# Mamba scan: y summed by tokens with accumulating fp32 transposes, the gate applied by tokens, and one token tile of each state scaled on VectorE

## The chip, the core and the metric

The kernel runs on one core of a Trainium2 chip. Its metric is the device time of one execution in microseconds (us). TensorE multiplies and transposes, VectorE (DVE in the rows), ScalarE (ACT) and GpSimd (POOL) work on 128 partitions at a time, SyncE (SP) issues the DMAs. PSUM, the memory that TensorE writes, has 8 banks of 512 fp32 per partition.

## The reference, cut to what matters

Two layers on x of 2 x 1024 x 256: attention and a gated feed-forward, then a Mamba block and a sparse feed-forward. The change is in the Mamba block, whose core is a scan over the 1024 tokens for each of 512 channels and 16 states:

```
x, z = split(h @ in_proj.T)                  # x, z: [b, 1024, 512]
x_conv = silu(conv4(x))
delta  = softplus(... + bias)                # [b, 1024, 512]
deltaA = exp(delta * A)                      # one A per channel and state
dBu    = delta * B[token, state] * x_conv
for each token:  h = deltaA * h + dBu ;  y = sum over the 16 states of h * C[token, state]
y = y + x_conv * D
y = y * silu(z)
out = y @ out_proj.T
```

## The kernel before, in words

Each engine has a program written out by hand; engines wait for each other by semaphores. After attention and the first feed-forward, each of the two batches b goes through `mamba_pre` (projections, convolution, softplus), `mamba_scan`, and a stretch behind the scan in which the output projection of b and the x projection of the next batch alternate. The sparse feed-forward comes last.

A scan works in channel tiles of 128 partitions x 1024 tokens. It has two halves of two channel tiles each (`half`, and `e` = 0, 1 inside it), and in each half 16 states, four (`v` = 0 to 3) in each of four iterations `it`. So a batch has 32 pairs of states; a pair is one state for both `e`. I call one (`v`, `e`) a step. A step passes through five operations:

- `spread` (ScalarE): u, kept by tokens in `m_uT` (tokens on partitions), is scaled by B of this state, one instruction of 256 channels for each of the 8 token tiles, into `m_uB`. One `spread` serves both `e`. Semaphore `ub_done`.
- `expand` (TensorE, L939): 8 transposes turn `m_uB` back to channels x tokens, into the PSUM banks 4+2e and 5+2e (`drive(e)`, one buffer for each `e`). It waits for the scan that read the same two banks. Semaphore `db_done`.
- `decays` (ScalarE, L1470): exp(delta * A) of 1024 tokens into `m_da`. Semaphore `da_done`.
- the scan (VectorE, L2238): h of 1024 tokens into one of the four `m_h` buffers, from `m_da` in SBUF and `drive(e)` in PSUM. Semaphore `scan_done`.
- the product with C (GpSimd, L2494), in place in `m_h`, semaphore `hc_done`; then `add_state` (TensorE, L946) adds it to y in PSUM by two matmuls of 512 columns with the identity as the weights (the trace has two records for each), banks 2e and 2e+1, semaphore `y_added`.

TensorE's order is `expand(v, e)`, `add_state(v-1, e)`, `expand(v, e+1)`, `add_state(v-1, e+1)`. When a half is done, VectorE forms y + D*x_conv (`dve_mamba_skip`, L2269), the product with silu(z) (`dve_mamba_gate`, L2275), ScalarE takes the high part (`act_y_hi`, L1504) and VectorE the low part (`dve_mamba_y_lo`, L2279) for the output projection `pe_mamba_out` (L984). For the first half these stand between the states of the second half; for the second half they come behind the scan.

## Time and profile before

| | us |
|---|---|
| median of 3 runs (1726.64 to 1728.74) | 1728.73 |
| the profiled execution, its own time | 1728.79 |
| its span in the trace | 1727.0 |
| first to last product with C, batch 0 | 1140.15 to 1312.79 |
| start of the sparse feed-forward on TensorE | 1577.21 |

Read it so: about 1.8 us lie outside the span. The two scans take a fifth of the span. Nothing ahead of 1108 us is touched by the change.

### The profile page before, as it was taken

Reading aid. Unit: us, or ns where it says so; the run is one execution under the profiler, and the core shown is the slowest. Engines: PE = TensorE matmul, PEld = TensorE weight load, DVE = VectorE, ACT = ScalarE, POOL = GpSimd, SP = SyncE. Lnnn points to the kernel's source line nnn. Section 1 sums busy time; section 2 is a strip of 40 time slices with the busy share of each in tenths; the row PEclk is TensorE's granted clock in tenths of the full one; section 3 lists DMA queues with packets and bytes.
Section 4 is the critical chain, followed back from the end, with each engine's and each line's share of the span. In section 5 each row is a group of like instructions: output and inputs, shape, how many; then the busy total and the mean of one; then the engine's idle time right before and its main releaser. Section 6 shows DMA issues by size and latency. Waiting matters only on the chain.

```text
span 1727.0 us, 31389 instructions
## 1 busy us (share of the span) xinstructions
PE 1649.3 (96%) x9564; PEld 1366.6 (79%) x9564; DVE 1394.7 (81%) x2319; ACT 1267.8 (73%) x2380; POOL 765.0 (44%) x717
## 2 busy tenths in 40 slices
PE   8999999999999999999997899789999899999998
PEld 7899889998999889989996788556557656557887
DVE  7788878887787778777876667878888788888997
ACT  5777777777777777777774555799996899984442
POOL 4444445443545354445442111059883079881000
PEclk9999999999999999999999999989999999999999
DMA  3000000000000000000000000023220022240000
GB/s 99 32 20 19 28 27 18 18 30 24 16 16 28 24 15 15 27 24 15 22 0 16 35 0 0 4 87 108 94 89 13 18 108 97 98 142 5 13 13 25
DMA packets 25105, 64.13 MB, mean 37 GB/s; under 512 B 2832, under 2 KB 8976, under 8 KB 24784
## 3 DMA queue, kind: packets, MB, share of 16 engines
q1 hardware_dynamic: 25040, 63.31, 10.8%
q8 instruction: 36, 0.59, 0.1%
q14 instruction: 29, 0.24, 0.0%
HBM read 60.94 MB, written 2.36 MB: 37 GB/s over the span
## 4 chain that ended last, share of the span: by engine, by line
PE 63%; POOL 18%; DVE 10%; issue 6%; ACT 2%; DMA 1%; POOLq 0%; DVEq 0%; SPq 0%; ACTq 0%
POOL m_h L2494 16%; PE ps L567 11%; PE ps L529 10%; PE ps L552 7%; PE ps L484 7%; PE ps L580 5%; PE ps L507 5%; PE ps L802 4%; PE ps L709 3%; PE ps L814 2%; PE ps L730 2%; POOL prob L2364 1%; PE ps L984 1%; POOL prob L2357 1%; DVE m_delta L2175 1%
## 5 line engine op out<-in xcount | busy, mean ns | idle before, releaser
L2494 POOL TENSOR_TENSOR m_h<-m_h,m_C 128x1024 f32<-128x1024 f32 x128 | 309.6, 2424 | 161.4 <-DVE m_h L2238 161.0
L2238 DVE TENSOR_TENSOR_SCAN m_h<-m_y,ps 128x1024 f32<-128x1024 f32 x128 | 291.0, 2283 | 44.9 <-PE ps L939 41.8
L2364 POOL TENSOR_SCALAR prob<-prob,rinv 128x128 f32<-128x128 f32 (+7 forms) x256 | 229.2, 903 | 212.7 <-DVE rinv L1655 206.2
L2357 POOL TENSOR_SCALAR prob<-prob 128x128 f32<-128x128 f32 (+7 forms) x256 | 188.4, 736 | 285.5 <-ACT prob L1077 277.0
L946 PE MATMUL ps<-m_h,ident 128*128 128x512 f32 x512 | 246.0, 603 | 11.2 <-POOL m_h L2494 11.1
L1621 DVE TENSOR_TENSOR pt_lo<-ps,pt_hi 128x512 fp32r<-128x512 f32 (+2 forms) x320 | 189.4, 604 | 81.0 <-ACT pt_hi L1090 79.2
L1614 DVE CUSTOM_DVE_ANT_0 prob<-prob,bias 128x128 f32<-128x128 f32 (+7 forms) x256 | 213.9, 853 | 7.9 <-POOL prob L2357 4.7
L1077 ACT ACTIVATE prob<-ps 128x128 f32<-128x128 f32 (+7 forms) x256 | 165.9, 653 | 67.2 <-PE ps L529 66.6
L1090 ACT ACTIVATE pt_hi<-ps 128x512 fp32r<-128x512 f32 (+2 forms) x320 | 162.9, 531 | 66.5 <-PE ps L552 64.5
L1464 ACT ACTIVATE m_u<-m_uT,m_bT 128x256 f32<-128x256 f32 x512 | 210.7, 497 | 0.1
L1083 ACT ACTIVATE prob<-prob,nmax 128x128 f32<-128x128 f32 (+7 forms) x256 | 198.2, 776 | 3.0 <-DVE nmax L1614 2.0
L939 PEld LDWEIGHTS ps<-ident,m_u 128*128 128x128 f32 x1024 | 122.6, 143 | 74.0 <-issue 59.8
L552 PE MATMUL ps<-ident,prob 128*128 128x128 f32 x1152 | 159.5, 274 | 7.4 <-POOL prob L2364 4.2
L552 PEld LDWEIGHTS ps<-ident,prob 128*128 128x128 f32 x1152 | 135.3, 141 | 29.2 <-issue 7.2
L946 PEld LDWEIGHTS ps<-m_h,ident 128*128 128x128 f32 x512 | 88.1, 192 | 79.8 <-issue 63.8
L529 PE MATMUL ps<-qk_hi 128*128 128x512 f32 (+2 forms) x384 | 143.4, 373 | 4.5 <-DVE v_lo L1627 2.4
L939 PE MATMUL ps<-ident,m_u 128*128 128x128 f32 x1024 | 136.4, 277 | 7.1 <-DVE m_uT L2226 5.0
L1470 ACT ACTIVATE m_y<-m_delta,negA 128x1024 f32<-128x1024 f32 x128 | 139.3, 1137 | 0.0
L529 PE MATMUL ps<-qk_hi,qk_lo 128*128 128x512 f32 (+2 forms) x384 | 131.9, 344 | 0.0
L529 PE MATMUL ps<-qk_lo,qk_hi 128*128 128x512 f32 (+2 forms) x384 | 131.3, 342 | 0.0
L567 PE MATMUL ps<-pt_hi,v_hi 128*128 128x512 f32 (+2 forms) x320 | 116.4, 364 | 0.0
L567 PE MATMUL ps<-pt_lo,v_hi 128*128 128x512 f32 (+2 forms) x320 | 115.7, 362 | 0.0
(263 smaller groups left out, 3960.2 us busy)
## 6 DMA issues: line engine op xcount, KB each, us to landing
m_C<-bc_dram SPq DMA_DIRECT2D x64, 512.0 KB, 3.6
wqk_raw<-wqk_in SPq DMA_DIRECT2D x16, 512.0 KB, 3.2
wv_raw<-wv_in SPq DMA_DIRECT2D x16, 256.0 KB, 2.6
wo_raw<-wo_in SPq DMA_DIRECT2D x16, 256.0 KB, 2.8
q_raw<-wgu_in SPq DMA_DIRECT2D x8, 256.0 KB, 2.7
raw<-wgu_in SPq DMA_DIRECT2D x1, 2048.0 KB, 8.1
out<-x SPq DMA_DIRECT2D x8, 256.0 KB, 2.1
x<-x_in SPq DMA_DIRECT2D x2, 512.0 KB, 4.4
```

The costliest lines, as they stand in the source:

```text
L529: mm = nc.tensor.matmul(flat[:, o + lo_c:o + hi_c], (qk_hi, qk_lo)[a][:, 2 * u, qt * P:(qt + 1) * P], (qk_hi, qk_lo)[w][:, 2 * u + 1, lo_c ...
L552: mm = nc.tensor.transpose(ps[:, 4 + idx % 2, r * P:(r + 1) * P], prob[:, at:at + P], ident[:, :])
L567: mm = nc.tensor.matmul(ps[:, 6 + g, c0:BANK], (v_hi, v_lo)[w][:, j, u * DH:(u + 1) * DH], cols, start=(j == 0 and i == 0), stop=(j == 4 * ...
L939: mm = nc.tensor.transpose(ps[:, 4 + 2 * e + t // 4, (t % 4) * P:(t % 4 + 1) * P], m_uB[:, v % 2, t, e * P:(e + 1) * P], ident[:, :])
L946: mm = nc.tensor.matmul(ps[:, 2 * e + c, :], ident[:, :], m_h[:, 2 * (v % 2) + e, c * BANK:(c + 1) * BANK], start=begin, stop=end)
L1083: nc.scalar.activation(prob[:, at:at + n], prob[:, at:at + n], ACT.Exp, bias=nmax[:, k:k + 1], scale=-1.0, accum_out=rsum[:, k:k + 1]).the ...
L1464: nc.scalar.activation(m_uB[:, v % 2, t, :], m_uT[:, half, t, :], ACT.Copy, scale=m_bT[:, t, bass.ds(it * RING + v, 1)]).then_inc(ub_done, 1)
L1614: nc.vector.tensor_tensor_reduce(out=tile, in0=tile, in1=bias[:, k // 8, S - n:S], scale=-1.0, scalar=BIG, op0=ALU.add, op1=ALU.min, accum ...
L2238: nc.vector.tensor_tensor_scan(m_h[:, 2 * (v % 2) + e, :], m_da[:, 2 * (v % 2) + e, :], drive(e), 0.0, ALU.mult, ALU.add).then_inc(scan_do ...
L2357: nc.gpsimd.tensor_scalar(prob[:, at:at + n], prob[:, at:at + n], CLIP, -CLIP, ALU.min, ALU.max).then_inc(s_clipped, 1)
L2364: nc.gpsimd.tensor_scalar(prob[:, at:at + n], prob[:, at:at + n], rinv[:, k:k + 1], 1.0, ALU.mult, ALU.mult).then_inc(norm_done, 1)
L2494: nc.gpsimd.tensor_tensor(state, state, m_C[:, v, :], ALU.mult).then_inc(hc_done, 1)
```

## The change

**What it does.** y is summed by tokens. `add_state` is now 8 transposes (tokens x 128 channels) that accumulate in PSUM (`is_transpose=True`, `start=False`), into blocks `y_block(t, e)` that fill banks 0 to 3. Ahead of them `begin_y` puts D*x_conv there by 8 transposes for each `e`; the product D*x_conv is made by GpSimd in four instructions at the start of `pool_mamba_scan`. silu(z) is made by tokens: `pe_in_z` has the x tokens as the weights. The gate is one multiplication of PSUM by `m_zT` for two banks, after both `e` are complete. Then `pe_y_turn` turns y back by 8 transposes for each channel tile into PSUM, from which ScalarE takes the high part and VectorE the low part. `spread` makes 7 tiles; the eighth (`spread_last`) is made by VectorE.

```diff
             def add_state(half, it, v, e, end=False):
                 pe.wait_ge(hc_done, unit(b, half, it, v, e) + 1)
-                for c in range(2):
-                    mm = nc.tensor.matmul(ps[:, 2 * e + c, :], ident[:, :],
-                                          m_h[:, 2 * (v % 2) + e, c * BANK:(c + 1) * BANK],
-                                          start=begin, stop=end)
+                for t in range(TILES):
+                    mm = nc.tensor.matmul(y_block(t, e), m_h[:, 2 * (v % 2) + e, t * P:(t + 1) * P], ident[:, :],
+                                          start=False, stop=end and e == 1 and t % 2 == 1, is_transpose=True,
+                                          skip_group_check=True)
                 mm.then_inc(y_added, 1)
+            def begin_y(half):
+                for e in range(2):
+                    pe.wait_ge(xd_done, DT * b + 2 * half + e + 1)
+                    for t in range(TILES):
+                        nc.tensor.matmul(y_block(t, e), m_xc[:, 2 * half + e, t * P:(t + 1) * P], ident[:, :],
+                                         start=e == 0 and t % 2 == 0, stop=False, is_transpose=True,
+                                         skip_group_check=True)
...
+            for v in range(RING):
+                if v == 2:
+                    for e in range(2):
+                        pe.wait_ge(scan_done, unit(b, 1, 1, v, e) + 3)
+                        pe_y_turn(pe, b, e)
+                        add_state(1, 1, v - 1, e)
+                for e in range(2):
+                    if v == 2:
+                        pe.wait_ge(y_lo, DT * b + e + 1)
+                    expand(1, 1, v, e)
...
+        def pe_y_turn(pe, b, e):
+            at = y_bank(b, e)
+            for t in range(TILES):
+                mm = nc.tensor.transpose(ps[:, at + t // 4, (t % 4) * P:(t % 4 + 1) * P],
+                                         m_yT[:, e // 2, t, (e % 2) * P:(e % 2 + 1) * P], ident[:, :])
+            mm.then_inc(yt_full, 1)
...
-            pe_in_x(pe, 1, range(4))
-            pe.wait_ge(y_skip, DT)
-            pe_mamba_out(pe, 0, (0, 1))
+            pe_in_x(pe, 1, range(2))
+            pe.wait_ge(yz_done, 3)
+            pe_mamba_out(pe, 0, (0, 1), range(4))
+            pe.wait_ge(yz_done, 4)
+            pe_y_turn(pe, 0, 2)
+            pe.wait_ge(m_in_read, 16 + 4)
+            pe_y_turn(pe, 0, 3)
+            pe_mamba_out(pe, 0, (0, 1), range(4, TILES))
+            pe.wait_ge(y_lo, 3)
+            pe_in_x(pe, 1, range(2, 4))
+            pe_mamba_out(pe, 0, (2,))
+            pe.wait_ge(y_lo, 4)
             pe_in_x(pe, 1, range(4, 8))
-            pe_mamba_out(pe, 0, (2,))
             pe_mamba_out(pe, 0, (3,))
             pe_mamba_pre(pe, 1)
             pe_mamba_scan(pe, 1)
-            pe.wait_ge(y_skip, 2 * DT - 1)
+            pe.wait_ge(yz_done, 8)
+            pe_y_turn(pe, 1, 2)
+            pe_y_turn(pe, 1, 3)
+            pe.wait_ge(y_lo, 8)
             pe_sparse_turn(pe, 0)
...
-                for t in range(TILES):
+                for t in range(TILES - 1):
                     nc.scalar.activation(m_uB[:, v % 2, t, :], m_uT[:, half, t, :], ACT.Copy,
                                          scale=m_bT[:, t, bass.ds(it * RING + v, 1)]).then_inc(ub_done, 1)
...
+            def spread_last(half, it, v):
+                dve.wait_ge(db_done, unit(b, half, it, v, 0) + 2)
+                dve.sem_inc(seen, 1)
+                nc.vector.tensor_scalar(m_uB[:, v % 2, TILES - 1, :], m_uT[:, half, TILES - 1, :],
+                                        m_bT[:, TILES - 1, bass.ds(it * RING + v, 1)], None,
+                                        ALU.mult).then_inc(ub_last, 1)
...
+        def dve_mamba_gate(dve, b, half, c):
+            dve.wait_ge(y_added, 8 + (2 * b + half + 1) * HALF_UNITS)
+            nc.vector.tensor_tensor(m_yT[:, half, 4 * c:4 * c + 4, :],
+                                    ps[:, 2 * c:2 * c + 2, :].rearrange("p a (t n) -> p (a t) n", t=2),
+                                    m_zT[:, half, 4 * c:4 * c + 4, :], ALU.mult).then_inc(yz_done, 1)
...
         def pool_mamba_scan(pool, b):
+            for e in range(DT):
+                pool.wait_ge(m_sp, 5 * DT * b + 3 * DT + 2 * e + 2)
+                nc.gpsimd.tensor_scalar(m_xc[:, e, :], m_xc[:, e, :], skip_d[:, e:e + 1], None,
+                                        ALU.mult).then_inc(xd_done, 1)
```

**How the instructions move.** First TensorE at the start of a scan. In these rows `m_u` is the memory of `m_uB`, and a transpose has the data as its weights. Before:

```order
L939 MATMUL ps<-ident,m_u 128x128 [waits ub_done,scan_done,ut1_read]
L939 MATMUL ps<-ident,m_u 128x128 [waits ub_done] x7
L939 MATMUL ps<-ident,m_u 128x128 [waits scan_done]
L939 MATMUL ps<-ident,m_u 128x128 x7
L939 MATMUL ps<-ident,m_u 128x128 [waits ub_done,scan_done]
L939 MATMUL ps<-ident,m_u 128x128 [waits ub_done] x7
L946 MATMUL ps<-m_h,ident 128x512 [waits hc_done]
L946 MATMUL ps<-m_h,ident 128x512
```

And now, from the second row on:

```order
L967 MATMUL ps<-ident,m_u 128x128 [waits ub_done] x6
L967 MATMUL ps<-ident,m_u 128x128 [waits ub_last]
L967 MATMUL ps<-ident,m_u 128x128 [waits scan_done]
L967 MATMUL ps<-ident,m_u 128x128 x7
L985 MATMUL ps<-ident,m_xc 128x128 [waits xd_done]
L985 MATMUL ps<-ident,m_xc 128x128 x7
L985 MATMUL ps<-ident,m_xc 128x128 [waits xd_done]
L985 MATMUL ps<-ident,m_xc 128x128 x7
L967 MATMUL ps<-ident,m_u 128x128 [waits ub_done,scan_done]
L967 MATMUL ps<-ident,m_u 128x128 [waits ub_done] x6
L967 MATMUL ps<-ident,m_u 128x128 [waits ub_last]
L975 MATMUL ps<-ident,m_h 128x128 [waits hc_done]
```

Every sum of a step has gone from two matmuls of 512 columns to eight transposes of 128, and 16 transposes of D*x_conv stand ahead of the third `expand`.

Second, TensorE in the second half, at the turn of the first half's y (states 5 and 6 of the second half), now:

```order
L1048 MATMUL ps<-ident,m_xc 128x128 [waits scan_done]
L1048 MATMUL ps<-ident,m_xc 128x128 x7
L975 MATMUL ps<-ident,m_h 128x128 [waits hc_done]
L975 MATMUL ps<-ident,m_h 128x128 x7
L1048 MATMUL ps<-ident,m_xc 128x128 [waits scan_done]
L1048 MATMUL ps<-ident,m_xc 128x128 x7
L975 MATMUL ps<-ident,m_h 128x128 [waits hc_done]
L975 MATMUL ps<-ident,m_h 128x128 x7
L967 MATMUL ps<-ident,m_u 128x128 [waits ub_done,scan_done,y_lo]
```

The two turns write the banks of `drive(0)` and `drive(1)`, so the next `expand` stands behind `y_lo`. Before, nothing of y passed through TensorE here.

Third, VectorE around the first half's y. Before:

```order
L2238 SCALAR_TENSOR_TENSOR m_h<-m_y,ps 128x1024 [waits db_done,y_added,da_done] x6
L2275 TENSOR_TENSOR m_xc<-m_xc,m_z 128x1024 [waits y_skip]
L2238 SCALAR_TENSOR_TENSOR m_h<-m_y,ps 128x1024 [waits db_done,y_added,da_done] x4
L2275 TENSOR_TENSOR m_xc<-m_xc,m_z 128x1024 [waits y_skip]
L2238 SCALAR_TENSOR_TENSOR m_h<-m_y,ps 128x1024 [waits db_done,y_added,da_done] x4
L2279 TENSOR_TENSOR m_yl<-m_xc,m_yh 128x1024 [waits y_hi]
```

And now (L2326 is the scan, L2333 the eighth tile of `spread`, L2384 the gate, L2390 the low part):

```order
L2326 SCALAR_TENSOR_TENSOR m_h<-m_y,ps 128x1024 [waits db_done,y_added,da_done] x2
L2384 TENSOR_TENSOR m_xc<-ps,m_z 128x1024 [waits y_added] x2
L2333 TENSOR_SCALAR m_u<-m_uT,m_bT 128x256 [waits db_done]
L2326 SCALAR_TENSOR_TENSOR m_h<-m_y,ps 128x1024 [waits db_done,y_added,da_done] x2
L2333 TENSOR_SCALAR m_u<-m_uT,m_bT 128x256 [waits db_done]
```

Two scans of a pair now have a `spread_last` between them and the next pair, the gates stand together and read PSUM, and (not shown) the two low parts stand together behind state 5.

## Rows read from the trace of the kernel before

**Rows 1.** The page's first line.

```profile
span 1727.0 us, 31389 instructions
```

**Rows 2.** Busy time by engine in a stretch; after the engines the granted clock.

```profile
1160.00:1200.00 40.00, 40.00 (x184) 24.22 (x183) 35.30 (x16) 40.00 (x77) 36.67 (x16) 1.00 0.31 105
```

**Rows 3.** Timeline of one loop in batch 0: start us, duration us, instruction.

```profile
1199.00 2.29 DVE L2238 TENSOR_TENSOR_SCAN m_h<-m_y,ps 128x1024 f32<-128x1024 f32 x1 [0.31 <-PE ps L939]
...
1201.36 2.37 POOL L2494 TENSOR_TENSOR m_h<-m_h,m_C 128x1024 f32<-128x1024 f32 x1 [0.23 <-DVE m_h L2238]
...
1203.91 1.88 PE L946 MATMUL ps<-m_h,ident 128*128 128x512 f32 x4
...
1205.63 1.04 PE L939 MATMUL ps<-ident,m_u 128*128 128x128 f32 x8
...
1206.51 1.88 PE L946 MATMUL ps<-m_h,ident 128*128 128x512 f32 x4
...
1206.77 2.29 DVE L2238 TENSOR_TENSOR_SCAN m_h<-m_y,ps 128x1024 f32<-128x1024 f32 x1 [0.31 <-PE ps L939]
```

**Rows 4.** Timeline of ScalarE, batch 0.

```profile
1222.27 3.29 ACT L1464 ACTIVATE m_u<-m_uT,m_bT 128x256 f32<-128x256 f32 x8
...
1225.47 2.17 ACT L1470 ACTIVATE m_y<-m_delta,negA 128x1024 f32<-128x1024 f32 x2
```

**Rows 5.** Timeline of VectorE: scans without a wait, and a low part among scans.

```profile
1229.10 6.75 DVE L2238 TENSOR_TENSOR_SCAN m_h<-m_y,ps 128x1024 f32<-128x1024 f32 x3
...
1278.08 1.38 DVE L2279 TENSOR_TENSOR m_yl<-m_xc,m_yh 128x1024 fp32r<-128x1024 f32 x1
```

**Rows 6.** The chain, GpSimd's products around that low part.

```profile
1276.01 2.22 POOL m_h L2494
...
1278.33 3.35 POOL m_h L2494
...
1281.73 2.17 POOL m_h L2494
1284.05 2.38 POOL m_h L2494
```

**Rows 7.** Groups by form: VectorE's scaling of one tile of 256.

```profile
L1559 DVE TENSOR_SCALAR m_uT<-x,mv,rstd 128x256 f32<-128x256 f32 x8 | 2.7, 407 | 0.2 <-POOL rstd L2349 0.2
```

**Rows 8.** Timeline of GpSimd: first and last product of batch 0's scan, last of batch 1's.

```profile
1140.15 2.36 POOL L2494 TENSOR_TENSOR m_h<-m_h,m_C 128x1024 f32<-128x1024 f32 x1 [51.38 <-DVE m_h L2238]
...
1310.44 2.35 POOL L2494 TENSOR_TENSOR m_h<-m_h,m_C 128x1024 f32<-128x1024 f32 x1 [0.25 <-DVE m_h L2238]
...
1557.40 2.39 POOL L2494 TENSOR_TENSOR m_h<-m_h,m_C 128x1024 f32<-128x1024 f32 x1 [0.25 <-DVE m_h L2238]
```

**Rows 9.** Groups by form: GpSimd's scaling of 1024 elements.

```profile
L2364 POOL TENSOR_SCALAR prob<-prob,rinv 128x1024 f32<-128x1024 f32 x32 | 36.1, 1129 | 17.1 <-DVE rinv L1655 17.1
```

**Rows 10.** Timeline of TensorE ahead of batch 0's scan, the transposes of u.

```profile
1126.93 6.27 PE L924 MATMUL ps<-ident,m_u 128*128 128x128 f32 x32 [0.94 <-ACT m_z L1442]
```

**Rows 11.** The chain behind batch 0's scan.

```profile
1314.82 5.49 PE ps L848 x24
...
1331.53 5.05 PE ps L984 x42
...
1336.60 0.69 DVE x L1898
```

**Rows 12.** Timeline of VectorE: convolution of a tile; ahead of the sparse feed-forward.

```profile
1330.87 3.92 DVE L2175 SCALAR_TENSOR_TENSOR m_delta<-m_xp,vecs,m_delta 128x1024 f32<-128x1024 f32 x3
...
1571.22 5.89 DVE L2286 TENSOR_TENSOR gu_lo<-raw,gu_hi 128x1024 fp32r<-128x1024 f32 x3
```

**Rows 13.** Busy time by stretch, as in rows 2: transposes alone, and a thinly used TensorE.

```profile
1128.00:1132.00 4.00, 4.00 (x21) 4.00 (x20) 3.25 (x3) 2.93 (x5) 0.00 (x0) 0.50 0.00 0
1132.00:1133.00 1.00, 1.00 (x10) 0.95 (x8) 0.00 (x0) 0.97 (x2) 0.00 (x0) 0.90 0.02 8
937.00:951.00 14.00, 10.34 (x102) 9.02 (x101) 7.67 (x15) 4.14 (x8) 0.95 (x2) 1.00 0.22 79
```

More of the change, by code:

```diff
@@ L951, in pe_mamba_scan @@
             last = DN // RING - 1
-            for half in range(2):
+            for e in range(2):
+                expand(0, 0, 0, e)
+            begin_y(0)
+            for v in range(1, RING):
                 for e in range(2):
-                    expand(half, 0, 0, e)
-                    if half:
-                        add_state(0, last, RING - 1, e, end=True)
-                for v in range(1, RING):
+                    expand(0, 0, v, e)
+                    add_state(0, 0, v - 1, e)
@@ L958, in pe_mamba_scan @@
+            with pe.Fori(1, last + 1) as it:
+                for v in range(RING):
                     for e in range(2):
[L959 to L970 removed]
+                        expand(0, it, v, e)
+                        if v:
+                            add_state(0, it, v - 1, e)
+                        else:
+                            add_state(0, it - 1, RING - 1, e)
@@ new lines, in pe_mamba_scan @@
+            for e in range(2):
+                expand(1, 0, 0, e)
+                add_state(0, last, RING - 1, e, end=True)
+            for e in range(2):
+                expand(1, 0, 1, e)
+            pe.wait_ge(yz_done, 4 * b + 2)
+            begin_y(1)
+            for e in range(2):
+                add_state(1, 0, 0, e)
+            for v in range(2, RING):
+                for e in range(2):
+                    expand(1, 0, v, e)
+                    add_state(1, 0, v - 1, e)
+            for v in range(RING):
+                if v == 2:
+                    for e in range(2):
+                        pe.wait_ge(scan_done, unit(b, 1, 1, v, e) + 3)
+                        pe_y_turn(pe, b, e)
+                        add_state(1, 1, v - 1, e)
+                for e in range(2):
+                    if v == 2:
+                        pe.wait_ge(y_lo, DT * b + e + 1)
+                    expand(1, 1, v, e)
+                    if v != 2:
+                        add_state(1, 1 if v else 0, (v - 1) % RING, e)
@@ L971, in pe_mamba_scan @@
+            with pe.Fori(2, last + 1) as it:
+                for v in range(RING):
+                    for e in range(2):
+                        expand(1, it, v, e)
+                        if v:
+                            add_state(1, it, v - 1, e)
+                        else:
+                            add_state(1, it - 1, RING - 1, e)
             for e in range(2):
@@ L2251, in dve_mamba_scan, with both @@
-            for v in range(RING):
-                state(1, 1, v)
+            def spread_last(half, it, v):
[4 more added lines that the diff above has]
+                                        ALU.mult).then_inc(ub_last, 1)
+            def both(half, it, v):
+                if v < RING - 1:
+                    spread_last(half, it, v + 1)
+                state(half, it, v)
@@ new lines, in dve_mamba_scan @@
+            last = DN // RING - 1
+            dve.wait_ge(ut0_read, 2 * (b + 1))
+            dve.wait_ge(bt_read, b + 1)
+            spread_last(0, 0, 0)
+            with dve.Fori(0, last) as it:
+                for v in range(RING):
+                    if v == RING - 1:
+                        spread_last(0, it + 1, 0)
+                    both(0, it, v)
+            dve.wait_ge(ut1_read, 2 * (b + 1))
+            for v in range(RING):
+                if v == RING - 1:
+                    spread_last(1, 0, 0)
+                both(0, last, v)
@@ L2253, in dve_mamba_scan @@
+            for v in range(RING):
+                if v == RING - 1:
+                    spread_last(1, 1, 0)
+                both(1, 0, v)
+                if v == 0:
+                    for c in range(2):
+                        dve_mamba_gate(dve, b, 0, c)
+            for v in range(RING):
+                if v == RING - 1:
+                    spread_last(1, 2, 0)
+                both(1, 1, v)
                 if v == 1:
-                    dve_mamba_gate(dve, b, 1)
-                if v == 3:
@@ L2256, in dve_mamba_scan @@
                     dve_mamba_y_lo(dve, b, 0)
+                    dve_mamba_y_lo(dve, b, 1)
             for v in range(RING):
-                state(1, 2, v)
-                if v == 1:
-                    dve_mamba_y_lo(dve, b, 1)
+                if v == RING - 1:
+                    spread_last(1, 3, 0)
+                both(1, 2, v)
                 if v == 3 and b == B - 1:
                     dve_sparse_stats(dve, 0)
-            with dve.Fori(3, DN // RING) as it:
+            with dve.Fori(last, DN // RING) as it:
```

104 lines of the change are left out of this document (46 added, 58 removed).

## The prediction

> **What bounds the kernel now.** I read the page for the span [rows 1], then the busy time by stretch in the scan [rows 2], one loop in the timeline [rows 3], and what ScalarE, VectorE and GpSimd do where nothing holds them [rows 4 to 7]. The reader is to see that in the scan no single engine is far ahead of the others: from 1160 to 1200 us TensorE and ScalarE are busy all the time, GpSimd 36.7 of 40 us, VectorE 35.3 [rows 2].
>
> The early part of the scan is held by a closed loop. A scan takes 2.29 us, 0.07 later GpSimd starts its product (2.37), 0.18 later TensorE's sum starts; its four records hold TensorE for 1.72 (1203.91 to 1205.63), then comes the `expand` of the next step (1.04), and 0.10 later the scan [rows 3]. From 1199.00 to 1206.77 that is 7.77 us, and the loop serves three steps, so 2.59 a step, 5.18 a pair. TensorE's own work is as long: the sum 1.72 and the `expand` 0.88 (1205.63 to 1206.51) make 2.60. ScalarE is slower than both in the long run: 8 tiles last 3.20 (1222.27 to 1225.47), or 0.40 each, and two decays, 2.17 long with about 0.09 of overlap, 2.08: 5.28 a pair [rows 4]. GpSimd's products run from 1140.15 to 1310.44 + 2.35, 172.64 us for 32 pairs [rows 8], 5.40 a pair; what is over 5.28 is the first half's y (two each of skip, gate, low part) and the start.
>
> **What each engine needs for a pair afterwards.**
> - TensorE: 32 transposes at 0.88/8 = 0.11 [rows 3] make 3.5 us. I take an accumulating transpose as long as `expand`'s, which has the same form.
> - ScalarE: one tile less, 5.28 - 0.40 = 4.88.
> - VectorE: scans that don't wait start (6.75 - 2.29)/2 = 2.23 apart at most [rows 5], 4.4 to 4.46 a pair, and `spread_last`. The nearest row is another scaling of 256 elements, 0.41 long with two scalars [rows 7]; I take 0.3 from start to next start. Together 4.75.
> - GpSimd: products without a wait start 1284.05 - 1281.73 = 2.32 apart [rows 6], 4.64 a pair. But GpSimd and VectorE get in each other's way: VectorE's low part starts at 1278.08 during a product that ends at 1278.23, lasts until 1279.46, and the product behind it takes 3.35 instead of 2.2 [rows 5, 6]. So VectorE waited for the product to end, and the next product waited for VectorE. Both of that subtraction's inputs are in SBUF.
>
> If `spread_last` behaves in that way, it is let in between two products once a pair, and GpSimd's pair is 4.64 + 0.33 = 4.97. VectorE then waits 0.2. The loop of three steps shrinks to 7.77 - (1.72 - 0.88) = 6.93, 4.62 a pair, and no longer decides. I take 4.97. From below a pair can't be under ScalarE's 4.88 (4.75 if its decays overlap better); from above, with no overlap at the hand-over, 4.64 + 0.41 + 0.10 = 5.15.
>
> The Trainium skill (SBUF — State Buffer, section "Who interferes with whom") says that GpSimd and a VectorE instruction that uses the shared port pair exclude each other for a whole instruction, and that issue order decides who blocks; it names `tensor_scalar` in its two-port mode. The rows above agree for a `tensor_tensor`; no row here settles it for `spread_last`. By a reading without this rule the pair would be ScalarE's 4.88.
>
> **The scan.** 32 x 4.97 = 159.0. To it comes the first half's y:
> - two gates behind the second half's first state, from PSUM, so they don't hold GpSimd; each about 1.2, as the low part's 1.38 less its wait of 0.15 [rows 5]: 2.35.
> - the turn. T is the end of the scan (state 5, e = 1). TensorE's turn of e = 0 is done before T; then it must wait for GpSimd's product, which ends at about T + 0.1, add (0.9), turn e = 1 (0.9): T + 2.1. ScalarE's high part takes about 1.1 (a decay of 1024 is as long), VectorE's low part 1.2: T + 4.6. VectorE's next scan is behind that and one `spread_last`, T + 4.9 instead of T + 0.3: 4.6. In it VectorE works 2.4 and waits 2.2.
> - `begin_y`: 16 transposes, 1.75, beside the first two scans; 0.1.
>
> Sum 166.05 against 172.64: -6.6 for a batch, -13.2 for two (the second batch taken as the first).
>
> **Around the scan, worse.**
> - Ahead of it GpSimd makes four products D*x_conv, about 1.1 each [rows 9], three of them beside VectorE's last softplus multiplications, which have two SBUF inputs. If GpSimd is let in first each time, u of the last channel tile comes 3.3 later; the transposes of u run 6.27 us at half clock and end at 1133.20 [rows 10], about 0.4 after they would have begun to wait, and run faster at full clock, which leaves 2.1. If VectorE is always first, 0. I take 1.0, for two batches +2.0.
> - Behind batch 0's scan TensorE is in the chain until 1331.53 + 5.05 [rows 11]. It has 16 transposes more (1.75), its last sum is 1.0 shorter: +0.7. But the x projection's second and later chunks come later, behind both turns and half of the output projection. Four chunks take 5.49, 42 records of the output projection 5.05 [rows 11], a convolution 3.92 [rows 12]. Counting from the last product: high parts end at 9.9, low parts at 11.2, the convolution of tile 0 at 15.1, tile 1 waits for chunk 3 (TensorE 14.1, ScalarE 1.3) and ends at 19.3, tile 2 waits for chunk 5 and ends at 25.0; four residuals of about 0.6 then end at 27.5, where the last ended about 1.4 behind 1336.60 [rows 11], 1338.0 - 1312.8 = 25.2. +2.3 (0.7 to 3).
> - Behind batch 1's scan the low parts wait for a longer row: both sums, both gates (T0 + 5.1, T0 the end of the last product), the turns behind the output projection's half (7.3), ScalarE's high part, a weight's high part (2.0, as VectorE's low parts of the same weights, 5.89/3) and the second high part (10.7), low part (12.0). TensorE now waits for it (`y_lo` 8) before it turns the first sparse rows (13.4), then ScalarE's 1.1 and VectorE's 0.7, and the weights' low parts, 5.89 [rows 12], which release the sparse feed-forward: T0 + 21.1, or 0.8 more with TensorE at half clock. It is at 17.4 now: 1571.22 + 5.89 and 0.1, less 1557.40 + 2.39 [rows 8, 12]. +4.2 (3 to 6).
>
> **Sum.** -13.2 + 2.0 + 2.3 + 4.2 = -4.7. Against the profiled execution's own 1728.8 (span 1727.0 and 1.8 outside it), which is within 0.1 of the median of the runs: 1724.1. A measurement of this kernel tells about 0.2%, 3.5 us, from no change.
>
> **The rivals.**
> - *TensorE's clock falls; slower.* TensorE would be used 3.5 us in 4.97, all of it in transposes. At 1.2 GHz they take 6.27/32 = 0.196 [rows 10], 32 of them 6.27, and TensorE is the bound: 64 pairs x (6.27 - 4.97) = +83, 1807. If it only comes and goes, half of that, about 1765. It ends slower than now from 12% of the scan at the low clock on. Against it: from 1128 to 1132 us TensorE did nothing but transposes, at 0.50, and the clock rose to full at 1132 in spite of that; from 937 to 951 it was busy 10.3 of 14 us, 74%, and the clock stayed at 1.00 [rows 13]. For it: no row has a long stretch of transposes alone at 70%. Chance 0.12, both versions together. The Trainium skill (TensorE: Matmul & The Clock Gate, Part 4) says that transposes don't count as a busy TensorE for the clock. By that rule the whole scan would be at half clock; the rise at 1132 speaks against it.
> - *GpSimd wins the hand-over.* If `spread_last` had to wait for a whole product more, 2.3 a pair, up to 64 x 2.3 = 147, 1870; if it happens in one pair of ten, +15, about 1739. Rows 5 and 6 show VectorE let in between two products, so 0.07.
> - *No change: the pair ends at 5.05 to 5.1.* A hand-over dearer by 0.08 to 0.13 costs 5 to 8 us and eats the gain: 1728 to 1732. The gain per batch is so thin that this needs no new mechanism. 0.22.
> - *ScalarE alone decides*, 4.88 or less: 64 x 0.09 = 6 more, with the cheap ends of the other terms 1712 to 1719. 0.14.
> - The forecast as summed, 0.45.
>
> **How the numbers follow.** The forecast's own range is 1719 to 1729. The range of 8 in 10 runs from the cheap end of ScalarE alone, 1711, into the rarer hand-over losses, 1742, and leaves out most of the clock's. Faster than 1725.3: ScalarE alone (0.14) and three quarters of the forecast (0.34), 0.48. Within 3.5 us: the rest of the forecast (0.11) and half of the third rival (0.11), 0.22. Slower: 0.30.
>
> **What the changed profile would show.** Steps right: GpSimd's products 2.3 to 2.4 apart with one of about 2.5 to 2.8 in each pair, behind a `spread_last`; VectorE's scans with under 0.3 of wait; the sum's records 0.11 apart; granted clock 1.00 through the scan; one gap of about 2 us on VectorE at the turn; from first to last product 166 us. Wrong: a clock of 0.50 in the scan; `spread_last` of 2 us; accumulating transposes longer than those of `expand`; a sparse start later than 22 us behind the last product.

## The result, and the profile after

The changed kernel takes 1716.09 us (median of 4, 1715.56 to 1717.52), the kernel before 1728.42 beside it (4, 1726.64 to 1728.74): ratio 0.9933, interval 0.9922 to 0.9945. That is 12.3 us less where 4.7 were forecast. The profiled execution took 1715.56 us. Its page, the span and three groups of the scan (busy us and mean ns behind the first bar, idle time and its releaser behind the second):

```profile
span 1713.8 us, 32643 instructions
...
L2604 POOL TENSOR_TENSOR m_h<-m_h,m_C 128x1024 f32<-128x1024 f32 x128 | 303.5, 2393 | 28.4 <-DVE m_h L2326 25.9
L2326 DVE TENSOR_TENSOR_SCAN m_h<-m_y,ps 128x1024 f32<-128x1024 f32 x128 | 285.2, 2266 | 3.6 <-PE ps L967 3.2
...
L975 PE MATMUL ps<-ident,m_h 128*128 128x128 f32 x1024 | 139.3, 279 | 57.4 <-POOL m_h L2604 57.4
```

Busy time by stretch, the one of [rows 2] and both scans whole (the last three numbers are granted clock, DMA share and GB/s):

```profile
1160.00:1200.00 40.00, 33.09 (x271) 29.32 (x272) 40.00 (x25) 40.00 (x74) 39.61 (x17) 1.00 0.30 105
...
1145.00:1300.00 155.00, 124.08 (x1008) 108.95 (x1008) 151.00 (x95) 144.67 (x265) 146.47 (x63) 1.00 0.27 95
1385.00:1539.00 154.00, 122.91 (x999) 107.82 (x997) 151.72 (x102) 144.16 (x265) 143.48 (x61) 1.00 0.35 116
```

The places have changed: TensorE, full in [rows 2], has 33.1 of 40 us, and VectorE, with 35.3 there, is never idle. One pair of states in the timeline, where [rows 3] stood:

```profile
1193.56 9.54 POOL L2604 TENSOR_TENSOR m_h<-m_h,m_C 128x1024 f32<-128x1024 f32 x4
...
1195.58 0.50 DVE L2333 TENSOR_SCALAR m_u<-m_uT,m_bT 128x256 f32<-128x256 f32 x1
...
1196.01 4.45 DVE L2326 TENSOR_TENSOR_SCAN m_h<-m_y,ps 128x1024 f32<-128x1024 f32 x2
...
1198.36 1.09 PE L975 MATMUL ps<-ident,m_h 128*128 128x128 f32 x8 [0.41 <-POOL m_h L2604]
...
1198.36 2.37 POOL L2604 TENSOR_TENSOR m_h<-m_h,m_C 128x1024 f32<-128x1024 f32 x1
...
1200.38 0.50 DVE L2333 TENSOR_SCALAR m_u<-m_uT,m_bT 128x256 f32<-128x256 f32 x1
...
1200.80 2.27 DVE L2326 TENSOR_TENSOR_SCAN m_h<-m_y,ps 128x1024 f32<-128x1024 f32 x1
```

The two `spread_last` start 1200.38 - 1195.58 = 4.80 us apart, and so do the scans behind them (1200.80 - 1196.01): a pair takes 4.80, not the 5.18 of [rows 3] nor the forecast 4.97. GpSimd's four products last 9.54 together, 2.39 each with what lies between them, and TensorE's sum waits for them. The loop can be read off the rows: the scan of `e` = 0 starts at 1196.01, its product at 1198.36, the product ends at 1200.73, `spread_last` 0.15 later (1200.88), and the next scan of `e` = 0 has started at 1200.80.

Ahead of the scan, VectorE and GpSimd:

```profile
1121.26 1.23 DVE L2311 TENSOR_TENSOR m_u<-m_delta,m_xc 128x1024 f32<-128x1024 f32 x1
...
1122.59 13.32 POOL L2595 TENSOR_SCALAR m_xc<-m_xc,vecs 128x1024 f32<-128x1024 f32 x4 [35.09 <-DVE m_u L2311]
...
1123.78 2.02 DVE L2311 TENSOR_TENSOR m_u<-m_delta,m_xc 128x1024 f32<-128x1024 f32 x1
...
1140.56 2.37 POOL L2604 TENSOR_TENSOR m_h<-m_h,m_C 128x1024 f32<-128x1024 f32 x1 [4.65 <-DVE m_h L2326]
```

The multiplication for u takes 1.23 alone and 2.02 beside GpSimd's D*x_conv, three times in each batch: 3 x 0.79 = 2.4 us. GpSimd's four products take 3.33 each. Behind batch 1's scan, where [rows 8] and [rows 12] stood:

```profile
1539.82 2.40 POOL L2604 TENSOR_TENSOR m_h<-m_h,m_C 128x1024 f32<-128x1024 f32 x1
...
1544.80 2.35 DVE L2384 TENSOR_TENSOR m_xc<-ps,m_z 128x1024 f32<-128x1024 f32 x2 [5.14 <-PE ps L975]
...
1547.47 1.91 PE L1048 MATMUL ps<-ident,m_xc 128*128 128x128 f32 x16
...
1552.46 1.23 DVE L2390 TENSOR_TENSOR m_yl<-ps,m_yh 128x1024 fp32r<-128x1024 f32 x1 [0.91 <-ACT m_yh L1591]
1553.74 1.68 PE L800 MATMUL ps<-ident,g_xn 128*128 128x128 f32 x8 [4.35 <-DVE m_yl L2390]
...
1563.12 0.73 PE L819 MATMUL ps<-g_xh,gu_hi 128*128 128x512 f32 x2 [1.00 <-DVE gu_lo L2398]
```

From the last product's end (1542.22) to the sparse feed-forward (1563.12) it is 20.9 us, forecast 21.1, before 17.4.

The spans differ by 13.2 us. From first to last product the scans take 160.2 and 162.4 us where they took 172.6 and 173.5: -12.4 and -11.1. Ahead of batch 0's scan +1.7, between the scans (1300.76 to 1379.83, before 1312.79 to 1386.29) +5.6, at the end +3.5, the rest of the sparse part +0.9, and -1.3 ahead of the Mamba part, where nothing was changed. Such a -1.3 belongs to the execution and not to the kernel: in the 14 traces of this case, whose code is the same up to there, the first convolution of the Mamba part starts anywhere from 1070.1 (`no_d`) to 1074.4 us (`mid_psum`), behind 10.2 and 20.5 us at the low clock. Below, I therefore compare stretches and not only whole times.

### The profile page after: what moved, and what is told of

It is laid out like the page before. It is cut to its first block, busy times and chain, and to the rows that moved or that the text cites. A ratio compares the mean times of both kernels' runs of the same rounds, so it can differ in the third digit from the quotient of the medians.

```text
span 1713.8 us, 32643 instructions
## 1 busy us (share of the span) xinstructions
PE 1580.6 (92%) x10204; PEld 1401.9 (82%) x10204; DVE 1407.4 (82%) x2375; ACT 1242.4 (72%) x2316; POOL 784.4 (46%) x725
## 4 chain that ended last, share of the span: by engine, by line
PE 63%; POOL 17%; DVE 10%; issue 6%; ACT 3%; DMA 1%; POOLq 0%; DVEq 0%; SPq 0%; ACTq 0%
POOL m_h L2604 15%; PE ps L584 11%; PE ps L546 11%; PE ps L569 7%; PE ps L501 7%; PE ps L597 5%; PE ps L524 5%; PE ps L819 4%; PE ps L726 3%; PE ps L831 2%; PE ps L747 2%; POOL prob L2470 1%; PE ps L897 1%; POOL prob L2463 1%; DVE m_delta L2263 1%
## 5 line engine op out<-in xcount | busy, mean ns | idle before, releaser
L2604 POOL TENSOR_TENSOR m_h<-m_h,m_C 128x1024 f32<-128x1024 f32 x128 | 303.5, 2393 | 28.4 <-DVE m_h L2326 25.9
L2326 DVE TENSOR_TENSOR_SCAN m_h<-m_y,ps 128x1024 f32<-128x1024 f32 x128 | 285.2, 2266 | 3.6 <-PE ps L967 3.2
L975 PE MATMUL ps<-ident,m_h 128*128 128x128 f32 x1024 | 139.3, 279 | 57.4 <-POOL m_h L2604 57.4
L1551 ACT ACTIVATE m_u<-m_uT,m_bT 128x256 f32<-128x256 f32 x448 | 185.1, 495 | 0.7 <-PE ps L967 0.5
L975 PEld LDWEIGHTS ps<-ident,m_h 128*128 128x128 f32 x1024 | 109.8, 140 | 86.4 <-POOL m_h L2604 86.2
L967 PEld LDWEIGHTS ps<-ident,m_u 128*128 128x128 f32 x1024 | 118.6, 143 | 11.7 <-DVE m_uT L2314 5.5
```

The costliest lines, as they stand in the source:

```text
L967: mm = nc.tensor.transpose(ps[:, 4 + 2 * e + t // 4, (t % 4) * P:(t % 4 + 1) * P], m_uB[:, v % 2, t, e * P:(e + 1) * P], ident[:, :])
L975: mm = nc.tensor.matmul(y_block(t, e), m_h[:, 2 * (v % 2) + e, t * P:(t + 1) * P], ident[:, :], start=False, stop=end and e == 1 and t % 2 ...
L2326: nc.vector.tensor_tensor_scan(m_h[:, 2 * (v % 2) + e, :], m_da[:, 2 * (v % 2) + e, :], drive(e), 0.0, ALU.mult, ALU.add).then_inc(scan_do ...
L2604: nc.gpsimd.tensor_tensor(state, state, m_C[:, v, :], ALU.mult).then_inc(hc_done, 1)
```

## The experiments

Four theories stand at the start. **Loop**: a pair is scan, product, `spread_last` held until the product ends, scan; of this GpSimd loses only about 0.14 us to the scaling. **ScalarE**: seven tiles and two decays, 4.87 us, decide. **VectorE**: its own time decides. **One half**: the summing alone or the tile alone made the gain.

**One half of the change at a time.** `f8_scalar` keeps the summing by tokens and gives all eight tiles back to ScalarE:

```diff
-                for t in range(TILES - 1):
+                for t in range(8):
                     nc.scalar.activation(m_uB[:, v % 2, t, :], m_uT[:, half, t, :], ACT.Copy,
...
-                nc.vector.tensor_scalar(m_uB[:, v % 2, TILES - 1, :], m_uT[:, half, TILES - 1, :],
```

> The changed kernel with all eight token tiles of each pair of states scaled on ScalarE again, and no scaling on VectorE in the scans. Theory: with eight tiles ScalarE (16 operations would be 8 x 0.66 us = 5.28 us a pair, from its 4.62 us of seven tiles and two copies scaled up in the trace after) bounds the loop, above the 4.79 us that the loop takes now; 64 pairs x 0.45 to 0.49 us = 29 to 31 us more than the changed kernel, so 1743 to 1748 us, slower than the kernel before too. Rival (ScalarE has slack, the gain is all from the summing by tokens): within 5 us of the changed kernel, 1711 to 1721 us.

Measured 1728.92 us (10 runs), before beside it 1728.17: ratio 1.0005, interval 0.9995 to 1.0015. No gain is left. Its timeline:

```profile
1196.78 4.46 DVE L2324 TENSOR_TENSOR_SCAN m_h<-m_y,ps 128x1024 f32<-128x1024 f32 x2 [0.81 <-ACT m_y L1555]
...
1197.54 3.29 ACT L1549 ACTIVATE m_u<-m_uT,m_bT 128x256 f32<-128x256 f32 x8
...
1200.73 2.17 ACT L1555 ACTIVATE m_y<-m_delta,negA 128x1024 f32<-128x1024 f32 x2
...
1201.95 4.46 DVE L2324 TENSOR_TENSOR_SCAN m_h<-m_y,ps 128x1024 f32<-128x1024 f32 x2 [0.71 <-ACT m_y L1555]
...
1202.81 3.28 ACT L1549 ACTIVATE m_u<-m_uT,m_bT 128x256 f32<-128x256 f32 x8
```

ScalarE's tiles start 1202.81 - 1197.54 = 5.27 us apart, and VectorE waits for its decays: the mechanism is as expected. The size is not: 12.8 us more than the changed kernel, not 29 to 31. ScalarE may run ahead of the scans, and the gates and turns, in which the scans stand still, give that lead back: the first five pairs of batch 0's scan come 4.4 to 5.1 us apart, those behind its gates and turn mostly 4.4 to 5.1, and the others 5.2 to 5.3. Where ScalarE doesn't hold it, a pair here is also shorter than the changed kernel's 4.80, as it has no `spread_last`. I had multiplied a steady pace by all 64 pairs.

`g_before_tile` is the kernel before with the tile moved alone (`spread_last` and its place in the order, as in the change). 

> The kernel before with the scaling of the last token tile moved to VectorE alone; the summing, gate and turns stay as they were. Theory: the pair was bound at 5.18 us by the loop from TensorE's expansion to the product and back and by TensorE's summing of y at two passes, not by ScalarE, so the move alone gives little: 1720 to 1729 us. Rival (ScalarE was the bound before, the move is what gave the gain): the pair falls to 4.8 us, 64 x 0.38 = 24 us less, 1704 us or even below the changed kernel.

Measured 1750.85 us (4 runs), before 1728.17: ratio 1.0132, interval 1.0115 to 1.0149; 1.3% slower, clear of the noise, where the theory had 1720 to 1729 and the rival 1704. In the first half a pair keeps its 5.19, as the theory had it: there the loop through TensorE decides and not ScalarE. The loss is in the second half, behind the gates and low parts by channels; GpSimd and VectorE there:

```profile
1259.19 1.20 DVE L2315 TENSOR_TENSOR m_xc<-m_xc,m_z 128x1024 f32<-128x1024 f32 x1
...
1259.35 3.26 POOL L2534 TENSOR_TENSOR m_h<-m_h,m_C 128x1024 f32<-128x1024 f32 x1 [0.62 <-DVE m_h L2246]
...
1260.31 2.46 DVE L2253 TENSOR_SCALAR m_u<-m_uT,m_bT 128x256 f32<-128x256 f32 x1
...
1262.69 4.45 DVE L2246 TENSOR_TENSOR_SCAN m_h<-m_y,ps 128x1024 f32<-128x1024 f32 x2
```

The gate, with both inputs in SBUF, ends at 1260.39; the product issued behind it then has the way, and `spread_last`, an operation of 0.33, takes 2.46: until 0.16 behind the product's end. Of its 64 records 10 are over 1.5 us, 22.7 us together, of which some 19 are waiting: four stand behind a gate and four behind a low part (2.46 each), two behind y + D*x_conv (1.5 each). The two halves of the change are worth nothing and minus 23 us alone, and 12 us together: each removes what hides the other's gain, and in the changed kernel, where the gates and the low parts read PSUM, only one `spread_last` record is over 0.7 us.

**What the tile on VectorE costs.** `n7_none` drops VectorE's scaling and `n6_none` one of ScalarE's as well:

```diff
-                nc.vector.tensor_scalar(m_uB[:, v % 2, TILES - 1, :], m_uT[:, half, TILES - 1, :],
+                return
...
+                for t in range(7, TILES):
+                    nc.vector.tensor_scalar(m_uB[:, v, t, :], m_uT[:, 0, t, :],
```

> The changed kernel without VectorE's scaling in the scans: tile 7 is written once a scan and then stays, so the output is not the reference's in its tokens. ScalarE still makes seven tiles. Theory (the loop scan, product, scaling, scan binds, and ScalarE lies just behind it with 4.87 us a pair in the stretch read): the scaling's time goes and ScalarE becomes the bound, 4.70 to 4.87 us a pair, so 1710 to 1720 us, little or nothing below the changed kernel. Rival (GpSimd and VectorE alone bind, ScalarE has slack): 4.65 us a pair, 64 x 0.14 = 9 us less, 1707 us.

> The changed kernel with ScalarE on six tiles, VectorE on none; tiles 6 and 7 are written once a scan and stay (the output is not the reference's there). Theory: nothing but the scans and products is left, two products at 2.33 us or two scans at 2.26 to 2.28 us with their starts, 4.62 to 4.67 us a pair; 64 x 0.12 to 0.17 us = 8 to 11 us below the changed kernel, 1705 to 1708 us, that is the whole price of the one tile on VectorE. Rival (something else, TensorE's 33 of 40 us or the two shared buffers, sets 4.79 us): within 2 us of the changed kernel.

Measured 1706.66 (ratio 0.9873, interval 0.9857 to 0.9889) and 1706.91 us (0.9881, 0.9864 to 0.9897), before 1728.17. In the first:

```profile
1194.60 13.93 DVE L2327 TENSOR_TENSOR_SCAN m_h<-m_y,ps 128x1024 f32<-128x1024 f32 x6
1194.72 14.04 POOL L2605 TENSOR_TENSOR m_h<-m_h,m_C 128x1024 f32<-128x1024 f32 x6
...
1199.86 2.91 ACT L1552 ACTIVATE m_u<-m_uT,m_bT 128x256 f32<-128x256 f32 x7
...
1204.73 2.91 ACT L1552 ACTIVATE m_u<-m_uT,m_bT 128x256 f32<-128x256 f32 x7
```

GpSimd's products now start (14.04 - 2.37)/5 = 2.33 us apart, 4.66 a pair. ScalarE still needs 1204.73 - 1199.86 = 4.87 with seven tiles, and yet taking one of them away changes nothing: over a half its lead covers the difference. Only at the end of the first half does `n7_none` show the lead used up, with pairs of 4.80 and 4.87 in batch 0 and one of 4.82 in batch 1, where `n6_none` keeps 4.65. So the ScalarE theory falls for the changed kernel, and the price of the tile on VectorE is 1716.1 - 1706.7 = 9.4 us, 0.147 a pair. `n6_none`, which decides this, came as expected; for `n7_none` it was the rival's number that came.

`n6_two` gives VectorE two tiles and ScalarE six:

```diff
-                for t in range(TILES - 1):
+                for t in range(6):
...
+                for t in range(6, 8):
+                    nc.vector.tensor_scalar(m_uB[:, v % 2, t, :], m_uT[:, half, t, :],
```

> The changed kernel with six tiles on ScalarE and two on VectorE. Theory A (VectorE's own time sets the pair): 4.80 + 0.28 us = 5.08 us, 64 x 0.28 = 18 us more, 1732 to 1735 us. Theory B (the second scaling meets GpSimd's next product, which took the port between the two, as the 2.46 us records in the second half of the kernel before with one tile moved): 2.3 us more in each pair, about 7.1 us a pair, 64 x 2.3 = 147 us more, 1850 to 1870 us. Where the first scaling is held until the product ends and the next product is already queued, B can hold for some pairs alone; a time between says in how many.

Measured 1846.91 us, before 1727.6: ratio 1.0687, interval 1.067 to 1.0703. The scaling's records (shortest, median, longest) and one pair:

```profile
L2334 DVE TENSOR_SCALAR m_u<-m_uT,m_bT x128: 341/494/2461, 1137.5 to 1661.3; 128x256 f32<-128x256 f32 x128
```

```profile
1227.79 2.25 DVE L2326 TENSOR_TENSOR_SCAN m_h<-m_y,ps 128x1024 f32<-128x1024 f32 x1
1229.96 2.86 DVE L2334 TENSOR_SCALAR m_u<-m_uT,m_bT 128x256 f32<-128x256 f32 x2
1232.74 4.45 DVE L2326 TENSOR_TENSOR_SCAN m_h<-m_y,ps 128x1024 f32<-128x1024 f32 x2
1237.12 2.86 DVE L2334 TENSOR_SCALAR m_u<-m_uT,m_bT 128x256 f32<-128x256 f32 x2
```

A pair takes 1237.12 - 1229.96 = 7.16 us. The first scaling slips in when a product ends; by the second the next product has begun, and it waits for that one whole. That is theory B, with 131 us more than the changed kernel where 147 were said: only 55 of the 128 records are over 1.5 us. VectorE's own time is refuted as what prices a second scaling; what counts is whether a product is under way. The Trainium skill (SBUF — State Buffer, section "Who interferes with whom") describes it so: whichever of the two starts first has the shared ports for its whole instruction. The 2.46 us records agree; GpSimd's D*x_conv, in the last section, doesn't.

**What makes the hold.** `strided` reads and writes the same tile with every second element first; `mid_sbuf` puts the scaling between the two scans of a state; `mid_psum` does that too and reads PSUM (the values are then not those of u). The edits, cut to their core: first `strided`, then `mid_psum`'s input, then the place in both `mid` versions.

```diff
-                nc.vector.tensor_scalar(m_uB[:, v % 2, TILES - 1, :], m_uT[:, half, TILES - 1, :],
+                nc.vector.tensor_scalar(m_uB[:, v % 2, TILES - 1, :].rearrange("p (i j) -> p j i", j=2),
+                                        m_uT[:, half, TILES - 1, :].rearrange("p (i j) -> p j i", j=2),
...
-                nc.vector.tensor_scalar(m_uB[:, v % 2, TILES - 1, :], m_uT[:, half, TILES - 1, :],
+                nc.vector.tensor_scalar(m_uB[:, v % 2, TILES - 1, :], ps[:, 6, 0:2 * P],
...
+                state(half, it, v, (0,))
                 if v < RING - 1:
                     spread_last(half, it, v + 1)
-                state(half, it, v)
+                state(half, it, v, (1,))
```

> The changed kernel with one edit: VectorE reads and writes the same last token tile with every second element first (the same values to the same places, in another order), so that its innermost step is two elements instead of one. Theory (the scaling is held until GpSimd's product ends because both want one port to SBUF, and a contiguous fp32 SBUF to SBUF scaling is of the kind that wants it): with steps of two it is no longer of that kind, the record of the scaling falls from 0.50 us to 0.33 to 0.40 us, GpSimd starts its products as soon as the scans are done, and a pair falls from 4.80 to 4.65 to 4.70 us; 64 x 0.10 to 0.15 us = 6 to 10 us below the changed kernel, 1706 to 1710 us. Rival 1 (the hand-over is a cost of semaphores and queues, or every VectorE operation on SBUF takes the port): record 0.50 us, pair 4.80 us, 1715 to 1717 us. Rival 2 (the strided form is slower by itself): pair 4.9 to 5.0 us, 1722 to 1729 us.

> The changed kernel with VectorE's scaling of the last tile moved between the two scans of a state and reading its input from PSUM instead of SBUF (the tile's values are then not those of u, so this part of the output is left out; the size and the output buffer are the same). Theory (one port to SBUF is held): with the input in PSUM nothing is held, record 0.33 to 0.40 us, pair 4.65 to 4.75 us, 1706 to 1712 us. Rival (hand-over by semaphores, or VectorE's own time is the bound): pair 4.80 us or more, 1716 us or more.

> The changed kernel with VectorE's scaling of the last tile moved between the two scans of a state, its input in SBUF as before: the control for the version that read it from PSUM. Theory (one port to SBUF, held by GpSimd's product for its whole length; the product of the scan before is over when the next scan is): the hand-over is the same at this place, 4.80 us a pair, 1715 to 1717 us. Rival (the place matters: here the scaling meets a product that has just begun): 4.80 + 2.3 us a pair, above 1800 us.

Measured 1715.42 (before 1727.6; 0.9927, 0.9913 to 0.994), 1723.55 (before 1727.6; 0.9971, 0.996 to 0.9982) and 1714.42 us (before 1726.46; 0.9928, 0.9913 to 0.9943). Their scaling records, in that order, each from its own kernel:

```profile
L2333 DVE TENSOR_SCALAR m_u<-m_uT,m_bT x64: 331/504/1209, 1136.3 to 1531.1; 128x256 f32<-128x256 f32 x64
```

```profile
L2333 DVE TENSOR_SCALAR m_u<-ps,m_bT x64: 456/483/485, 1138.9 to 1540.8; 128x256 f32<-128x256 f32 x64
```

```profile
L2333 DVE TENSOR_SCALAR m_u<-m_uT,m_bT x64: 320/500/519, 1136.1 to 1531.7; 128x256 f32<-128x256 f32 x64
```

With a step of two elements nothing changes, so my idea that the contiguous form alone is held falls. The place in the order doesn't matter either, 4.80 a pair. From PSUM the scaling takes 0.46 at the least, even where GpSimd waits, and a pair takes 4.75 to 4.92 with VectorE all but always busy (39.77 of 40 us from 1160 to 1200): the pair alone doesn't tell whether the hold is gone. The records speak for it. GpSimd's product right behind a scaling takes 2.42 us in the changed kernel, in `mid_sbuf` and in `strided`, where its others take 2.37; in `mid_psum` it takes 2.37 like the others. And the scaling itself grows beside the end of a product from 0.33 or 0.34 to 0.50 with its input in SBUF, but only from 0.46 to 0.48 in PSUM. No run puts such a scaling where a product has just begun, which would show it outright. The 7.5 us that `mid_psum` takes more than the changed kernel aren't all its pairs' either: its trace is 3.0 us later ahead of the Mamba part, and two pairs at the low clock cost it 1.2 us each.

**GpSimd's D*x_conv.** Three versions make some of the four products wait until VectorE's softplus is done (all four in `h_late`, whose edit is shown, three in `h_one`, two in `h_two`), and `no_d` leaves the products out, so that y begins from x_conv itself.

```diff
-                pool.wait_ge(m_sp, 5 * DT * b + 3 * DT + 2 * e + 2)
+                pool.wait_ge(m_sp, 5 * DT * (b + 1))
```

> The changed kernel, where GpSimd's four products of D and the convolved x wait until VectorE has finished the whole softplus. Theory: in the changed kernel three of VectorE's products of delta and x take 2.02 instead of 1.23 us beside them, 3 x 0.8 = 2.4 us in each batch on the way to the scan; waiting takes this away and the products end some 4.5 us later, still before they are wanted: 2 to 5 us less, 1711 to 1714 us. Rival (the start of the scan waits for GpSimd, whose work is then late): no change or up to 4 us more, 1716 to 1720 us.

> The changed kernel, where GpSimd makes its first product of D and the convolved x when it did, and the other three only once VectorE has finished the softplus. Theory: two of the three held products of delta and x become 1.23 instead of 2.02 us, 2 x 0.8 us a batch; three products at 2.83 us after the end of the softplus are over 8.5 us later, 1 us before GpSimd's first product with C can start: 2 x 1.6 = 3.2 us less, 1712 to 1714 us. Rival (as when all four waited, GpSimd is late for the scan): 1717 to 1720 us.

> The same with two products early and two late. Theory: one of the three holds goes, 2 x 0.8 = 1.6 us less, 1714 to 1715 us, with 3 us of room ahead of GpSimd's first product with C. Rival: no change, 1716 us.

> The changed kernel without GpSimd's product of D and the convolved x (y then begins from the convolved x itself; this part of the output is left out). It prices the product: theory, 2 x 2.4 = 4.8 us less and up to 1 us for a first product that starts sooner, 1710 to 1712 us. Rival (the stretch ahead of the scan is set by ScalarE and TensorE as well, so that VectorE's gain is lost to the next wait): 1713 to 1716 us.

Measured: `h_late` 1720.52 us (before 1727.6; 0.9956, 0.9943 to 0.997), `h_one` 1716.02 (before 1726.46; 0.9934, 0.992 to 0.9948), `h_two` 1717.06 (0.993, 0.9917 to 0.9944), `no_d` 1712.26 (0.9925, 0.9904 to 0.9946). In `h_late` the multiplications take 1.23 again, and the rival came:

```profile
1130.10 11.33 POOL L2595 TENSOR_SCALAR m_xc<-m_xc,vecs 128x1024 f32<-128x1024 f32 x4 [42.64 <-DVE m_u L2311]
...
1141.39 7.03 POOL L2604 TENSOR_TENSOR m_h<-m_h,m_C 128x1024 f32<-128x1024 f32 x3
...
1146.98 2.29 DVE L2326 TENSOR_TENSOR_SCAN m_h<-m_y,ps 128x1024 f32<-128x1024 f32 x1 [3.22 <-PE ps L967]
```

VectorE's first scans come 1.7 us sooner, but GpSimd starts its products 0.8 later than in the changed kernel, and the scans then wait: the second pair takes 7.9 us in batch 0 and 10.4 in batch 1 in place of 4.8. A part of that is the clock: TensorE, idle for 3.26 and 4.59 us before its first sums, is then granted the low clock, and the 8 transposes that the scan waits for take 1.91 and 1.92 us instead of 1.04.

Of the others, `no_d` came at the edge of the theory's 1710 to 1712, `h_one` between its theory (1712 to 1714) and its rival (1717 to 1720), and `h_two` beside the rival's 1716. From VectorE's first multiplication for u to GpSimd's first product with C it is 19.3 us in the changed kernel, 18.1 in `h_one` and 17.7 in `no_d` (17.6 in the kernel before): of the 2.4 us that the three held multiplications lose, D*x_conv costs this stretch 1.6 a batch. Counted from the start of the trace `no_d` would seem to win 2.95 (1137.61 against 1140.56), but 1.35 of that it has ahead of the Mamba part.

`h_one` starts sooner, and yet ends at the same time. Part of `no_d`'s gain gets lost, too: it wins 1.6 ahead of the first scan and 1.9 between the scans, and gives back 1.2 and 1.3 within them. For `no_d` the cause in batch 0 is behind the turn:

```profile
1249.98 1.09 PE L967 MATMUL ps<-ident,m_u 128*128 128x128 f32 x8 [1.36 <-DVE m_h L2326]
1250.01 4.74 POOL L2600 TENSOR_TENSOR m_h<-m_h,m_C 128x1024 f32<-128x1024 f32 x2 [4.54 <-DVE m_h L2326]
...
1252.42 1.83 PE L975 MATMUL ps<-ident,m_h 128*128 128x128 f32 x8 [1.35 <-POOL m_h L2600]
...
1254.05 1.91 PE L967 MATMUL ps<-ident,m_u 128*128 128x128 f32 x8
```

and in its busy time by stretch:

```profile
1250.00:1252.00 2.00, 1.07 (x8) 0.84 (x8) 2.00 (x1) 2.00 (x5) 1.99 (x1) 1.00 0.03 8
1252.00:1254.00 2.00, 1.58 (x8) 1.58 (x9) 2.00 (x3) 2.00 (x6) 2.00 (x2) 0.66 0.00 0
1254.00:1256.00 2.00, 2.00 (x12) 2.00 (x11) 0.71 (x1) 1.96 (x3) 1.96 (x2) 0.50 0.00 0
```

TensorE, idle for 1.36 and 1.35 us behind the turn, is granted 0.50, that is 1.2 of 2.4 GHz; its eight transposes take 1.91 instead of 1.04, and this pair takes 6.1 instead of 4.8 us. The changed kernel has the same two idle times there (1.36 and 1.34) and keeps 1.00. `h_one` loses 1.1 to 1.4 us in this way three times, at 1253, 1492 and 1523 us, 3.8 together, more than the 2.5 by which it had come sooner into its two scans. Whether a clock falls differs between executions: of `h_two`'s five, two took 1712.7 and 1713.0 us (mean granted clock 0.984 and 0.982) and three 1717.1 to 1717.7 (0.978 to 0.981). Its trace is of a long one, with falls at 1254 and 1524 us; so its theory of 1714 to 1715 is neither borne out nor refuted. By the medians, no version that computes the whole reference beats the changed kernel by more than a measurement tells.

## Why the prediction was right and wrong

The sign, the place and the mechanism of the gain were right, and 1716.1 lies in the range of 8 in 10; the forecast of 1724.1 was 8.0 too high. In the traces the scans are 10.3 us better than forecast, from one term of the sum, and the stretches around them 3.2 worse (+11.7 for +8.5); -1.3 lies where nothing was changed. That the range held is luck in part: 1716.1 is outside the forecast's own 1719 to 1729 and inside the 1712 to 1719 of the rival that ScalarE alone decides, and that rival isn't what happened.

- **The pair of states, the mis-sized term.** "If `spread_last` behaves in that way, it is let in between two products once a pair, and GpSimd's pair is 4.64 + 0.33 = 4.97." It is let in so, but costs 0.14: 4.80 a pair, against 4.66 without it in `n7_none` and `n6_none`. 64 x 0.17 = 10.9 us, and the two scans came out 10.3 shorter than forecast (-23.5, forecast -13.2). The 0.33 has no working in the prediction; it is nearly the scaling's whole length. The scaling (0.34 without a wait, 0.50 held) starts before the product ends and only its tail is in GpSimd's way. [rows 5] and [rows 6] had shown as much: the products around the low part start 1281.73 - 1278.33 = 3.40 apart instead of 2.32, so 1.08 was lost to an operation of 1.38 - 0.15 = 1.23, 0.15 less than its length. The same 0.15 off the scaling's 0.34 would have given 0.19.
- **TensorE.** "I take an accumulating transpose as long as `expand`'s": 279 and 278 ns a record; right. TensorE's busy time is 33.1 x 4.80/40 = 3.97 a pair, 0.5 over the 3.5 of the sum, without consequence. The loop of three steps through TensorE no longer decides; right, as pairs of 4.66 in `n7_none` show.
- **ScalarE at 4.88.** Its pace is 4.87, but as a lower bound it was wrong: `n7_none` runs at 4.66 with it, on a lead that the gates and turns give back. The rival that ScalarE alone decides, which would have been 4.88, falls for the same reason, though its times took in the result. With eight tiles it does decide (`f8_scalar`).
- **The gates, the turn.** 2.35 and 4.6 forecast; the pairs there take 7.14 and 9.23, that is 2.34 and 4.43 over a pair's 4.80. Right.
- **D*x_conv, +1.0 a batch.** VectorE's multiplications lost 2.4 a batch, of which 1.7 reached the first product. I put GpSimd's product at 1.1 from [rows 9]; it takes 2.8 alone and 3.3 here. `no_d` prices it at 1.6 and 1.9 us for the two batches, 3.5 together, of which its clock took 2.5 back; the medians differ by 3.8, of which some is the execution's.
- **The boundary, +2.3; the end, +4.2.** Of the 5.6 us between the scans, 2.1 are the longer way to the last residual (27.35 us behind the scan, forecast 27.5, before 25.2), 1.4 lie between that and batch 1's first multiplication for u, and 2.1 from there to the first product, where the multiplications were held. The end took +3.5, with the low clock from 1554.1 to 1557.5 in it, where TensorE turns the sparse rows (1.68 us where it took 1.32). What makes the +0.9 behind it isn't shown.
- **The clock.** The rival of a low clock throughout fell: 1.00 over both scans with TensorE 80% busy, all of it in transposes. By that, the rule of the Trainium skill (TensorE: Matmul & The Clock Gate, Part 4), that transposes don't count for the clock, isn't seen here. That it "only comes and goes" was priced far too high, at 40 us; where it did (in other versions' traces), it cost 1.0 to 1.4 us most times. The 12% of the scan from which the low clock was to lose the gain should have been 6%: 4.7 of 83 us.
- **GpSimd wins the hand-over.** Not in the changed kernel, where only one scaling is over 0.7 us. But it was one edit away: `n6_two` (+131 us) and `g_before_tile` (+23) are this rival. 0.07 was fair for this order of instructions, not for the neighbours.

What stays open: whether an input in PSUM frees the scaling from the hold outright (the records of `mid_psum` say so, no run tests it where a product has just begun); why GpSimd's product takes 2.8 us here and 1.1 in [rows 9]; and what decides whether the clock falls.

## What to carry to other kernels

A scaling of VectorE in SBUF beside a busy GpSimd costs little (0.14 us here) if it begins as a product ends, and a whole product (2.3 us here) if the next has begun: look at the order of both queues before counting its length, and allow one such operation behind a product, not two. Two edits can each be worthless alone, since each one's gain is hidden by what the other removes; price a part by taking it away from the whole as well as by adding it to the old. And an engine whose steady pace is over that of the loop needn't set it, if it may run ahead and the loop has stops in which the lead comes back.
